# Adding a group's sums one step later, with the next group's edge terms ahead of its sum products

## The reference, cut to what matters

```python
Qh, Kh, Vh = (x @ Wq.T + bq), (x @ Wk.T + bk), (x @ Wv.T + bv)     # as n x 4 x 16
Ee = edge_attr @ We.T + be                                         # as edges x 4 x 16
score = (Kh[src] * Qh[dst] * (1.0 / np.sqrt(D)) * Ee).sum(-1)
score = jnp.exp(jnp.clip(score, -5.0, 5.0))
msg = Vh[src] * score[..., None]
wV = jax.ops.segment_sum(msg, dst, num_segments=n)
```

## Time and profile before

| | before |
|---|---|
| median of 3 runs | 2643.93 us (2632.73 to 2664.64) |
| the profiled execution's own time | 2622.77 us |
| its span, first to last instruction | 2621.0 us |
| mean granted clock of PE, share of full speed | 0.744 |
| busy share of PE, DVE, ACT, POOL | 57%, 54%, 39%, 47% |

### The profile page before, as it was taken

One profiled execution on the slowest core, in us unless ns is written; L12 is line 12 of the kernel. 1 busy time (PEld: TensorE's weight loads), 2 busy tenths in 40 slices (PEclk: granted clock), 3 DMA queues, 4 the chain that ended last, 5 costly groups with the idle time before them and its releaser, 6 DMA issues. The chain is left out here.

```text
span 2621.0 us, 43664 instructions
## 1 busy us (share of the span) xinstructions
PE 1481.0 (57%) x12911; PEld 1234.8 (47%) x12911; DVE 1421.5 (54%) x3789; ACT 1011.9 (39%) x2229; POOL 1243.5 (47%) x1346
## 2 busy tenths in 40 slices
PE   4555555555555555555454586586103655556697
PEld 4444443434443443444343486475103645455586
DVE  6555554555555555555454787886202534344586
ACT  4333333333333333333233490591103533344575
POOL 5455555555555555555455191273764343444300
PEclk7777777777777777777777698696556777777898
DMA  4222222222222222222122120004111111111110
GB/s 130 52 58 58 56 59 54 60 57 57 58 58 58 55 59 58 58 57 56 52 59 55 39 67 22 1 2 125 35 24 25 36 34 38 34 42 32 35 34 14
DMA packets 112819, 128.69 MB, mean 49 GB/s; under 512 B 68447, under 2 KB 75923, under 8 KB 112426
## 3 DMA queue, kind: packets, MB, share of 16 engines
q0 software_dynamic: 35776, 62.74, 10.2%
q1 hardware_dynamic: 54842, 59.37, 7.8%
q10 hardware_dynamic: 22064, 4.85, 0.9%
HBM read 116.64 MB, written 10.20 MB: 48 GB/s over the span
## 5 line engine op out<-in xcount | busy, mean ns | idle before, releaser
L476 POOL DMA_INDIRECT shared<-kv_tab,idx x784 | 756.5, 965 | 668.0 <-DMA idx<-in_src 435.5
L875 PE MATMUL bank<-key_hot,lo_hot 128*128 128x350 f16 x784 | 218.7, 391 | 593.9 <-DVE count L635 399.1
L875 PEld LDWEIGHTS bank<-key_hot,lo_hot 128*128 128x128 f16 x784 | 57.5, 100 | 711.3 <-issue 699.2
L2455 POOL DMA_INDIRECT count<-att_tab,count x240 | 232.6, 969 | 261.4 <-PE bank L3009 156.0
L672 DVE TENSOR_TENSOR acc<-acc,bank 65x64 f32 x98 | 21.3, 218 | 486.2 <-remote 485.6
L751 ACT ACTIVATE expo<-score 128x32 f32<-128x32 f32 x98 | 22.5, 229 | 616.5 <-DVE score L653 609.9
L2837 ACT ACTIVATE shared<-shared 128x126 f32<-128x126 bf16 x336 | 143.6, 484 | 279.2 <-remote 175.6
L635 DVE TENSOR_TENSOR count<-count,bank 128x350 f32 x392 | 205.2, 523 | 81.6 <-issue 73.9
L741 ACT ACTIVATE lo_dist<-iota_neg,tile_lo 128x128 f16<-128x128 f32 x784 | 238.4, 390 | 0.0
L2986 PE MATMUL bank<-shared 128*128 128x150 f32 x896 | 156.7, 319 | 121.6 <-issue 56.2
L2986 PEld LDWEIGHTS bank<-shared 128*128 128x128 f32 x896 | 138.8, 208 | 146.2 <-issue 137.8
(11 more groups left out here) (539 smaller groups left out, 3235.6 us busy)
## 6 DMA issues: line engine op xcount, KB each, us to landing
shared<-in_edge_attr SPq DMA_DIRECT2D x97, 256.0 KB
shared<-lo_tab SPq DMA_DIRECT2D x28, 512.0 KB
shared<-kv_tab,idx POOLq DMA_INDIRECT x784
count<-att_tab,count POOLq DMA_INDIRECT x240
qwin<-q_tab ACTq DMA_DIRECT2D x196, 16.0 KB
g_edge<-att_tab,count POOLq DMA_INDIRECT x94
idx<-in_src SPq DMA_DIRECT2D x93, 4.0 KB, 1.5
dh_tab<-acc SPq DMA_DIRECT2D x1, 1176.0 KB
```

What stands on the lines that cost most here:

```text
L476: nc.gpsimd.indirect_dma_start(kv[:, s, c, :], None, kv_tab, bass.IndirectOffsetOnAxis(ap=of[:, s, c:c + 1], axis=0)).then_inc(kv_in[s], 16)
L875: last = nc.tensor.matmul(bank[6 + q % 2][:, 0:KC], lo_hot[:, c, :], key_hot[:, c, :], start=i == 0, stop=i == GT - 1)
L2455: nc.gpsimd.indirect_dma_start(ring[s][:, j, 0:D + 2], None, att_tab[1], bass.IndirectOffsetOnAxis(ap=src_i[:, t:t + 1], axis=0)).then_inc ...
```

## The change

Three edits, all in the loop of the first attention. DVE no longer adds a group's sums at the end of its step, but in the next step, right behind the first counts (the last group's are still added at the end of its own step). The offset of the sums gets its own register load. For this DVE's loop is written out instead of calling `pipelined`, with the first RS = 4 steps in front of the loop so that the very first has nothing to add. PE makes the edge terms of g + 1 ahead of the sum products of g; since bank 3 is still read by DVE for group g until its score is done, PE waits for `sc_ok` first. The query products stay behind the sum products.

```diff
+                    def add_sums(g, s):
+                        b = spans(dve, g)
+                        dve.wait_ge(sum_ok, j * G + g + 1)
+                        nc.vector.tensor_tensor(acc[0:D + 1, bass.ds(b, W)], acc[0:D + 1, bass.ds(b, W)], bank[5][0:D + 1, 0:W], ALU.add).then_inc(slot_free, 1)
...
-                        b, *group_at = nc.values_load_multi_w_load_instructions(
-                            base_i[0:1, bass.ds(g, 1), 0:1 + GG].rearrange("a g k -> a (g k)"), engines=[mybir.EngineType.DVE],
+                        group_at = nc.values_load_multi_w_load_instructions(
+                            base_i[0:1, bass.ds(g, 1), 1:1 + GG].rearrange("a g k -> a (g k)"), engines=[mybir.EngineType.DVE],
...
                         add_counts(0)
+                        if not first:
+                            add_sums(g - 1, (s - 1) % RS)
                         if after:
                             node_hots(*after)
...
                         if after:
                             key_hots(*after)
-                        dve.wait_ge(sum_ok, n)
-                        nc.vector.tensor_tensor(acc[0:D + 1, bass.ds(b, W)], acc[0:D + 1, bass.ds(b, W)], bank[5][0:D + 1, 0:W], ALU.add).then_inc(slot_free, 1)
+                        else:
+                            add_sums(g, s)
                         dve.drain()
...
-                    pipelined(dve, front, step)
+                    front(0, 0, 1)
+                    for g in range(RS):
+                        step(g, g, 1, (g + 1, (g + 1) % RS, (g + 1) // RS + 1))
+                    with dve.Fori(1, G // RS) as it:
...
@@ PE @@
                         if after:
                             turn_hots(*after)
+                            pe.wait_ge(sc_ok, n)
+                            pass_on(pe)
+                            edge_terms(*after)
                         pe.wait_ge(msg_ok, n)
                         for c in range(C):
                             last = nc.tensor.matmul(bank[5][0:D + 1, 0:W], msg[:, c, :], hots[:, s % 2, c, :], start=c == 0, stop=c == C - 1)
                         last.then_inc(sum_ok, 1)
                         if after:
-                            edge_products(*after)
+                            query_products(*after)
```

More of the change, by code:

```diff
@@ L625, in front @@
                         key_hots(g, s, m)
+                    def add_sums(g, s):
+                        b = spans(dve, g)
+                        dve.wait_ge(sum_ok, j * G + g + 1)
+                        nc.vector.tensor_tensor(acc[0:D + 1, bass.ds(b, W)], acc[0:D + 1, bass.ds(b, W)], bank[5][0:D + 1, 0:W], ALU.add).then_inc(slot_free, 1)
                     def step(g, s, m, after):
                         n = j * G + g + 1
+                        first = isinstance(g, int) and g == 0
                         def add_counts(q):
@@ L670, in step @@
                             key_hots(*after)
-                        dve.wait_ge(sum_ok, n)
-                        nc.vector.tensor_tensor(acc[0:D + 1, bass.ds(b, W)], acc[0:D + 1, bass.ds(b, W)], bank[5][0:D + 1, 0:W], ALU.add).then_inc(slot_free, 1)
+                        else:
+                            add_sums(g, s)
                         dve.drain()
-                    pipelined(dve, front, step)
+                    front(0, 0, 1)
+                    for g in range(RS):
+                        step(g, g, 1, (g + 1, (g + 1) % RS, (g + 1) // RS + 1))
+                    with dve.Fori(1, G // RS) as it:
+                        for s in range(RS):
+                            step(it * RS + s, s, it + 1, (it * RS + s + 1, (s + 1) % RS, it + 1 + (s + 1) // RS))
+                    for g in range(G - G % RS, G):
+                        step(g, g % RS, g // RS + 1, (g + 1, (g + 1) % RS, (g + 1) // RS + 1) if g + 1 < G else None)
             @block.scalar
@@ L843, in turn_hots, with edge_terms @@
                         last.then_inc(hot_t, 1)
-                    def edge_products(g, s, m):
+                    def edge_terms(g, s, m):
                         n = j * G + g + 1
@@ L854, in edge_products, with query_products @@
                         last.then_inc(ee_ok, 1)
+                    def query_products(g, s, m):
+                        n = j * G + g + 1
                         pe.wait_ge(hot_ts, n)
@@ L864, in front @@
                         turn_hots(g, s, m)
-                        edge_products(g, s, m)
+                        edge_terms(g, s, m)
+                        query_products(g, s, m)
                     def step(g, s, m, after):
```

## The result

The changed kernel takes 2894.34 us (median of 4 runs, 2869.18 to 2902.62) where the kernel before takes 2654.28 us beside it: ratio 1.090, 95% interval 1.079 to 1.101. It is slower, by about the 230 us forecast. The profiled execution took 2897.02 us, its span is 2895.2 us.

The account below looks back on a forecast made before the run. The slot-to-slot ring (sums, index load, eight gathers, landing) was taken to bound the step, growing from 14.40 to 16.90 us; 92 x 2.50 = 230 us on 2643.9 gives 2874, range 2740 to 2980.

Parts of the forecast that it names:

- What the wait is for: DVE's 5.20 us wait before the sums: not PE's arithmetic; finished PE work is told late while gathers are under way.
- The wait moves to L649: The 5.20 us before the sums aren't saved but move to DVE's query-term multiplication, becoming about 7 us.
- The ring: First attention's slot-to-slot cycle of sums, index load, eight gathers, landing sets the step; later sums lengthen it from 14.40 to 16.90 us.
- The edge terms in front of the sums cost nothing and aren't held: PE's edge terms moved ahead add no cost, and L641 with its 0.69 us runs before the release.
- 2.50 us from release to sums: On DVE, L649, reduction, clip and first counts take 2.25 us, plus 0.25 of register load; bounds 2.25 to 2.84.
- The sum: First attention's 92 steps at 2.50 us each add 230 us, giving 2874 for the median; bounds 2851 to 2905.
- DVE learns of everything at once when a batch has landed: In each step, PE's finished results are told late under gathers, then all at once after landing, 1.96 us behind the last.
- the rival: DVE's wait was really for the sums and vanishes: step 10.1 us, 396 us less, 2248; chance 0.13.

Follow-up runs that it names:

- the early indices: SyncE loads indices one step ahead, GpSimd waits for the slot: 0.959 on the kernel before, 0.954 on the changed kernel with sums added ahead of the query-term wait.
- the sums in front: Changed kernel with the sums added right in front of DVE's wait for the query terms: 1.011 to the kernel before, step 14.56 us.
- DVE's half alone: Kernel before with DVE adding the sums in the next step behind the first counts, PE's order as before: 1.094, step 16.91 us.
- the kernel with fills: Kernel before with keys and values brought by plain DMA and GpSimd filling an unread tile in place of gathers: 0.913, step 11.98 us.

## Why the prediction was right

- **What the wait is for.** Right: not PE's arithmetic. With half the gathers it is gone, with a plain DMA of the same bytes it is gone, and work taken off PE doesn't shorten the step.
- **The wait moves to L649** and is larger, about 7 us. Right: 7.82 us a step at L656.
- **The ring.** Right: gathers, index load and the distance from release to sums each go into the step at their full length or nearly, as the halved gathers in the changed kernel (5.02 us less from first to last), the early indices (1.96 and 1.7) and the moved sums (2.36 and 2.32) show. In the kernel before, the halved gathers don't show it: there the step came down to what DVE and PE need by themselves.
- **The edge terms in front of the sums cost nothing and aren't held.** Right for the second (0.3 us a step of idle time at L648, as at L641 before). By itself PE's order costs 0.19 us a step.
- **2.50 us from release to sums.** Found: 2.36. The multiplication, reduction, clip and counts were read rightly as 2.25; of the register load 0.11 is left, where I took 0.25. The mean step grew by 2.48 all the same: 2.32 by the moved sums (16.88 against 14.56 with the sums in front) and 0.16 by the rest of the change (14.56 against 14.40), which I had costed at nothing. Two small errors cancel.
- **The sum.** 230 us forecast, 228.1 found in the 92 steps. That the median is 2894 and not 2874 us isn't from the steps; the profiled executions have 41.9 us in the later stage. The forecast had no term for that stage; without them the time would have been some 2855, inside the range as well.
- **Too strong:** that DVE learns of everything at once when a batch has landed. In the kernel before it does (`ee_ok` 0.10 us after `sum_ok`, `qd_ok` 0.09 us later). The kernel with DVE's half alone has 1.50 us between edge terms and queries, and in the one with fewer sum products, results come through in the middle of a batch. "A batch under way delays what follows on PE's side by several microseconds" is as much as the runs carry. The forecast didn't need more, because in this kernel the late result is due behind the batch.

The rule of the Trainium skill that spoke for the rival (SBUF — State Buffer, SBUF: two separate sides) holds as far as it goes: the plain DMA of the same bytes slowed nothing (9.42 us against 9.37). By what way gathers from GpSimd's queue hold PE's semaphores stays open. The traces do show that PE itself is held too when the gathers go on for long: in the later stage of the changed kernel, from 2100 to 2176 us, its weight loads and products start one by one, 1.40 us apart (2161.59 and 2164.39 are two products with a weight load between them), though a product takes 0.37 us. Two rivals are untested. Other transfers from GpSimd's queue may do the same. And every execution here comes with the profiler's record of it, so no run tells whether PE is held as long without one.

## What to carry to other kernels

When an engine waits long for results that the trace shows done, look at what ends just before it goes on, and test that by taking it away, before moving the work that waits. In a ring of buffers, the instruction that frees the buffer belongs at the very moment of the release: each microsecond of other work put in front of it (here 2.36) is paid in every step, though every engine has slack. And freeing a buffer earlier isn't safe either: where batches of gathers then run into each other, the next results wait through both.

## What the runs showed of the hardware that I had not expected

- While GpSimd's gathers are under way PE's semaphores are updated late, by 5.77, 4.28 and 3.28 us in the kernel before, and DVE's and ACT's are not (0.01 us). Under 112 gathers in a row DVE waited 95 us in one kernel and 135 in another, and for 76 us of them PE started one instruction every 1.40 us.
- Four fewer gathers of GpSimd's queue a group take DVE's long wait away, and neither 256 KB by a plain DMA nor 8.9 us of GpSimd's fills a step brings it back.
- GpSimd's fills slow DVE's comparisons of 128x350 f16: 684 ns each in the kernel with fills, 317 ns in the kernel before, 313 in the changed one. The multiplications of 128x512 f32 keep their 0.69 us. The Trainium skill (GPSIMD Engine Reference, 1. Specifications) says that GpSimd's way to SBUF is shared with VectorE; for fills the trace agrees. Gathers don't do it: the 313 to 317 ns are beside them.
- Four of PE's sum products fewer a group made the kernel 5.4% slower, by moving the freeing of a slot in front of the end of a batch.
